# A cross-network recommendation kernel on one core: the first group's seven shifted-row loads in buffers of their own, and a changed order of waits around the scratch writes

## What is computed

```python
x = x0                                   # e: [512, 40, 16]
for k in (k0, k1, k2):                   # k0: [128,40,40], k1, k2: [128,128,40]
    x = jnp.einsum('bhd,bmd,ohm->bod', x, x0, k)
    outputs.append(jnp.sum(x, axis=-1))
z = jnp.concatenate(outputs, axis=1)
h = jnp.concatenate([z, dense_ctx], axis=1)
h = relu(h @ W_top1 + b_top1); h = relu(h @ W_top2 + b_top2)
y = h @ W_top3
```

## Time and profile before

| | |
|---|---|
| time before, median of 3 runs (lowest to highest) | 703.82 us (703.36 to 705.27) |
| the profiled execution: time, span | 706.33 us, 704.4 us |
| TensorE busy | 651.3 us, 92% of the span |
| VectorE busy | 619.2 us, 88% |
| ScalarE busy | 554.1 us, 79% |
| GpSimd busy | 321.0 us, 46% |
| start of the first layer 1 matmul | 41.48 us |
| mean granted TensorE clock | 0.995 of full speed |

### The profile page before, as it was taken

How to read it: one execution, slowest core, us unless ns; L and a number is a source line. 1 busy time by engine, 2 the same in 40 slices (tenths; PEclk the granted TensorE clock), 3 DMA queues, 4 the chain that set the end, 5 groups by cost and what they waited for, 6 DMA issues and landing times.

```text
span 704.4 us, 11705 instructions
## 1 busy us (share of the span) xinstructions
PE 651.3 (92%) x2502; PEld 463.7 (66%) x2502; DVE 619.2 (88%) x1355; ACT 554.1 (79%) x1950; POOL 321.0 (46%) x250
## 2 busy tenths in 40 slices
PE   0389999999989999999999999999999999999998
PEld 0157776776767777777667777777777767765573
DVE  2559999999999999999899999999999999988390
ACT  2158888888888988888788888898888898889383
POOL 6645564636364655556463647465545611110000
PEclk9989999999999999999999999999999999999999
DMA  6431212121312122221213130212222122400000
GB/s 212 115 88 49 76 46 80 45 80 33 92 21 56 53 52 72 50 74 46 80 34 91 31 89 22 62 48 51 74 49 75 45 79 65 174 3 0 30 2 0
DMA packets 56671, 43.00 MB, mean 61 GB/s; under 512 B 37007, under 2 KB 40335, under 8 KB 56352
## 3 DMA queue, kind: packets, MB, share of 16 engines
q1 hardware_dynamic: 51488, 41.08, 19.7%
q0 software_dynamic: 5120, 1.32, 2.3%
HBM read 40.41 MB, written 1.97 MB: 60 GB/s over the span
## 4 chain that ended last, share of the span: by engine, by line
PE 76%; DVE 14%; issue 5%; DMA 2%; POOL 1%; DVEq 1%; SPq 0%; ACT 0%
PE Y L572 17%; PE Y L574 16%; PE Y L573 16%; PE X L539 14%; DVE sums L487 4%; PE GB L546 4%; DVE sums L436 2%; DVE sums L431 2%; DVE sums L449 2%; PE X L610 1%; POOL x0g L288 1%; DMA pairs<-scratch 1%; DVE x1lo L420 1%; PE X L612 1%; PE X L611 1%
## 5 line engine op out<-in xcount | busy, mean ns | idle before, releaser
L372 ACT ACTIVATE sums<-Y,xtok 128x128 f32<-128x128 f32 x1792 | 493.4, 395 | 91.1 <-PE Y L574 91.0
L572 PE MATMUL Y<-k1lo,x1hi 128*128 128x512 f32 x640 | 315.5, 493 | 20.3 <-DVE sums L487 17.1
L574 PE MATMUL Y<-k1hi,x1lo 128*128 128x512 f32 x640 | 253.5, 396 | 0.0
L573 PE MATMUL Y<-k1hi,x1hi 128*128 128x512 f32 x640 | 252.8, 395 | 0.0
L487 DVE SCALAR_TENSOR_TENSOR sums<-Y,xtok,sums 128x128 f32<-128x128 f32 x768 | 229.4, 341 | 24.2 <-PE Y L574 21.9
L317 POOL TENSOR_TENSOR diag<-xtok,mask 128x320 f32<-128x320 f32 x64 | 103.9, 1624 | 267.2 <-PE GB L546 267.0
L288 POOL DMA_INDIRECT x0g<-in_table,rows_now x160 | 199.2, 1245 | 42.2 <-issue 38.6
L572 PEld LDWEIGHTS Y<-k1lo,x1hi 128*128 128x128 f32 x640 | 120.6, 188 | 82.2 <-DVE sums L487 27.8
L573 PEld LDWEIGHTS Y<-k1hi,x1hi 128*128 128x128 f32 x640 | 121.1, 189 | 50.6 <-issue 25.3
L539 PE MATMUL X<-pairs,w 120*128 120x512 f32 x224 | 116.9, 604 | 29.8 <-DVE pairs L416 29.8
L574 PEld LDWEIGHTS Y<-k1hi,x1lo 128*128 128x128 f32 x640 | 120.7, 189 | 29.2
(11 more groups left out here) (64 smaller groups left out, 249.3 us busy)
## 6 DMA issues: line engine op xcount, KB each, us to landing
pairs<-scratch SPq DMA_DIRECT2D x112, 240.0 KB
A<-scratch SPq DMA_DIRECT2D x16, 240.0 KB
k1raw<-in_k SPq DMA_DIRECT2D x1, 2560.0 KB, 10.6
x0g<-in_table,rows_now POOLq DMA_INDIRECT x160, 3.2
k2s<-in_k SPq DMA_DIRECT2D x1, 2560.0 KB, 9.1
scratch<-x0g SPq DMA_DIRECT2D x96, 20.0 KB, 1.7
pairs<-in_w SPq DMA_DIRECT2D x3, 256.0 KB, 3.0
w2s<-in_w SPq DMA_DIRECT2D x1, 512.0 KB, 4.0
```

Of the source, the lines that this page charges most:

```text
L372: ins = nc.scalar.activation(sums[tile % 2][:, k * O:(k + 1) * O], Y[(NCH * tile + c) % YB][:, i * O:(i + 1) * O], ACT.Copy, scale=xtok[sl ...
L572: nc.tensor.matmul(y, hi[:, tok], k1lo[:, cols], start=True, stop=False)
L573: nc.tensor.matmul(y, hi[:, tok], k1hi[:, cols], start=False, stop=False)
L574: nc.tensor.matmul(y, lo[:, tok], k1hi[:, cols], start=False, stop=True).then_inc(s_y, 1)
```

## The change

Four edits. (1) In `spread(0, -1)` the seven chunks of the first group are loaded into seven buffers `first0` to `first6`, which lie in bytes of `G` that are not yet in use, so SyncE waits for no matmul between them. (2) For the first group `A3` waits only for the four writes of rows 0 to 39; the two repeated pieces have a semaphore of their own (`s_again`), for which SyncE waits after it has issued `A3`. (3) For all later groups SyncE waits, ahead of the two writes of repeated rows (40 to 59), until all of layer 0 of the group before is done (`s_l0 >= NC0 * g`); `A3` and the chunks stand behind that wait. (4) `chunk` counts buffers from group 1 on, since the first group no longer uses `pairs`.

```diff
@@ def chunk
-    k = NC0 * (slot + 1) + c
-    return GPB * NC0 * u + k, k % NR, GPB * NC0 // NR * u + k // NR
+    number, k = NC0 * (GPB * u + slot + 1) + c, NC0 * slot + c
+    return number, k % NR, GPB * NC0 // NR * u + k // NR
@@ buffers
+        first = [over("G", f"first{c}", [P, GROUP], skip=4 * (NCH * BANK + 2 * NC0 * O + c * GROUP))
+                 for c in range(NC0)]
@@ SyncE, spread
-                for q in range(FQ):
-                    for first in range(q * GF, ROLLS, M):
-                        sp.dma_start(scratch[par, first:first + GF, :].rearrange("f (b d) -> b f d", d=D),
-                                     x0g[par][q * GS:(q + 1) * GS, :, :]).then_inc(s_scratch, 16)
-                sp.wait_ge(s_scratch, 16 * (ROLLS // GF) * (g + 1))
+                for row in range(0, ROLLS, GF):
+                    q = row % M // GF
+                    if row == M and slot >= 0:
+                        sp.wait_ge(s_l0, NC0 * g)
+                    sp.dma_start(scratch[par, row:row + GF, :].rearrange("f (b d) -> b f d", d=D),
+                                 x0g[par][q * GS:(q + 1) * GS, :, :]).then_inc(
+                                     s_again if slot < 0 and row >= M else s_scratch, 16)
+                sp.wait_ge(s_scratch, 16 * (ROLLS // GF * g + FQ))
                 sp.dma_start(A3[par][0:PR, :], rows(0, 0)).then_inc(s_a3, 16)
+                if slot < 0:
+                    sp.wait_ge(s_again, 16 * (ROLLS // GF - FQ))
                 for c in range(NC0):
+                    if slot < 0:
+                        sp.dma_start(first[c][0:PR, :], rows(KC * c, 1)).then_inc(s_first[c], 16)
+                        continue
                     n, buf, _ = chunk(u, slot, c)
-                    if slot >= 0 or c >= NR:
-                        sp.wait_ge(s_l0, n - NR + 1)
+                    sp.wait_ge(s_l0, n - NR + 1)
                     sp.dma_start(pairs[buf][0:PR, :], rows(KC * c, 1)).then_inc(s_roll[buf], 16)
@@ VectorE, prod steps (TensorE's l0 steps read the same buffer)
+                    if slot < 0:
+                        rolled = first[int(step[4:])]
+                        dve.wait_ge(s_first[int(step[4:])], 16)
+                    else:
+                        _, buf, fills = chunk(u, slot, int(step[4:]))
+                        rolled = pairs[buf]
+                        dve.wait_ge(s_roll[buf], 16 * (fills + 1))
+                    nc.vector.tensor_tensor(rolled[0:PR, :], rolled[0:PR, :], A3[par][0:PR, :],
                                             ALU.mult).then_inc(s_prod, 1)
```

More of the change, by code:

```diff
@@ L191, in build @@
         s_xtok = sem("xtok_ready")
-        s_scratch, s_a3 = sem("scratch_written"), sem("a3_in")
+        s_scratch, s_again, s_a3 = sem("scratch_written"), sem("scratch_written_again"), sem("a3_in")
+        s_first = [sem(f"first_in{c}") for c in range(NC0)]
         s_roll = [sem(f"rolled_in{i}") for i in range(NR)]
@@ L412, in prep @@
                 if step[:4] == "prod":
-                    _, buf, fills = chunk(u, slot, int(step[4:]))
                     dve.wait_ge(s_a3, 16 * (g + 1))
-                    dve.wait_ge(s_roll[buf], 16 * (fills + 1))
-                    nc.vector.tensor_tensor(pairs[buf][0:PR, :], pairs[buf][0:PR, :], A3[par][0:PR, :],
+                    if slot < 0:
[6 more added lines that the diff above has]
+                    nc.vector.tensor_tensor(rolled[0:PR, :], rolled[0:PR, :], A3[par][0:PR, :],
                                             ALU.mult).then_inc(s_prod, 1)
@@ L538, in prep @@
                     pe.wait_ge(s_prod, n + 1)
-                    nc.tensor.matmul(X1[:, :], w0[:, c * O:(c + 1) * O], pairs[buf][0:PR, :],
+                    rolled = pairs[buf] if slot >= 0 else first[c]
+                    nc.tensor.matmul(X1[:, :], w0[:, c * O:(c + 1) * O], rolled[0:PR, :],
                                      start=(c == 0), stop=(c == NC0 - 1)).then_inc(s_l0, 1)
```

## The result

The changed kernel took 708.97 us (median of 14 runs, 704.0 to 712.97) against 704.13 us for the kernel before (14 runs, 702.83 to 707.25). The ratio is 1.0056, with a 95% interval from 1.0035 to 1.0077. I had forecast 698.0 us. The start did become earlier, much as worked out; the time was lost in the middle, at a place that the prediction never looked at.

What follows compares the result with a forecast made beforehand. TensorE's list, with a little of VectorE's, was taken to bound the tiles. Seven buffers with early `A3` 4.6, clock 1.4, less 0.2 for the new wait, gave 5.8 us: from 703.8 to 698.0 us, range 697.0 to 701.3.

Steps and rivals of the forecast that it cites:

- What bounds the kernel: In the tiles TensorE's list sets the cost; time saved in the first 41 us moves everything forward one for one.
- Part 1: At the start, `A3` goes out at 20.8 and the first chunk at 21.8, 0.95 us earlier; the added wait is hidden.
- Part 2: In the first group, seven buffers make TensorE the limit; `l0_6` ends at 35.4 against 40.00, a gain of 4.6 us.
- Part 3: At the start of layer 1, TensorE no longer runs at half clock, a gain of 1.4 us; called the least certain step.
- the dip: TensorE's granted clock at 0.50 from 38 to 44.5 us in the profile before; its staying was a rival, chance 0.16.
- Part 4: In later groups, SyncE's new wait leaves 3.6 us to spare; only group 1 is charged, 0.1 to 0.2 us.
- The rival on the slower side: In 14 groups VectorE stands at `prod0` because `A3` and chunk 0 come late; 703 to 708 us, chance 0.05.

Runs made afterwards that it cites:

- e5: Changed kernel with the wait for layer 0 only in the first slot (slot 0) of a loop body; 708.62 us, ratio 1.004 to the kernel before.
- e10: Changed kernel without the wait for layer 0, plus five 240 KB copies that no product waits for, issued at the jump back; 708.07 us, ratio 1.0028.
- e12: The kernel before with the loop over bodies written out; 700.77 us, ratio 0.9937 to the kernel before.
- e2: The kernel before with only the wait for layer 0 ahead of the repeated rows added (scratch writes reordered to allow it); 712.09 us, ratio 1.0097.
- e1: Changed kernel without the wait for layer 0 ahead of the repeated rows, first group's `A3` with its own semaphore; 701.78 us, ratio 0.9954 to the kernel before.
- e4: Changed kernel with the wait for layer 0 in all slots of a loop body but the last; 709.45 us, ratio 1.0058 to the kernel before.
- e3: Changed kernel with the wait for layer 0 only in the last slot of a loop body, first group's `A3` with its own semaphore; 702.24 us, ratio 0.9955.
- e6: Changed kernel with the wait for layer 0 in slots 1 to 3 only, first group's `A3` with its own semaphore; 702.49 us, ratio 0.9949.
- e7: Changed kernel, all waits kept, with the loop over bodies written out four times; 697.61 us, ratio 0.9881 to the kernel before.
- e8: Changed kernel without the wait for layer 0 and with the loop over bodies written out; 698.87 us, ratio 0.9894 to the kernel before.
- e11: Changed kernel without the wait for layer 0, first group's `A3` waiting for all six scratch writes again; 703.22 us, ratio 0.9968 to the kernel before.

## Why the prediction was wrong

- **What bounds the kernel.** Right for the groups inside a body. Wrong in "unless the tiles themselves are disturbed" being left without a search: I looked at one later group (the one at 303 us) and took it for all 15. The two periods across a jump already stood out before, by 1.4 us each, and the very view of the earlier trace rows had an entry for them (waiter, releaser, total us, times, longest):

```profile
DVE sums L444 <- issue: 2.9, 2, 1.5
```

- **Part 1, early `A3`.** I had 20.8 and 21.8; the profile has 21.30 and 22.26, and `A3` in the other runs with this start lies between 20.43 and 21.31. Right in mechanism, and hidden as said. Its worth of 0.95 us was not told apart from noise.
- **Part 2, seven buffers.** TensorE was the limit of the start, without a gap, as said. (The 4.50 us that I called waiting for a load were the load's own; TensorE stood still for 2.26 us between its pairs. It doesn't enter the sum, which follows the ends of the pairs.) `l0_6` ended at 36.93 and not 35.4: half a microsecond from the landing of the scratch writes, and six pairs in 6.94 us where I had 5.9, since the clock rose later. In e5 they took 5.58 us and layer 1 began at 36.74; in e10 6.87 and 38.08. The moment of the rise differs from run to run, so this term has a spread of over 1 us.
- **Part 3, the dip.** It was gone in the changed kernel, so the term of 1.4 us held for these two profiles. But e12 and e2 keep the old start, with two waits for loads of about a microsecond, and begin layer 1 at 39.51 and 39.78 with the clock up. And of the 78 runs of the kernel before beside the experiments, 29 had a mean granted clock of 1.000, which leaves no room for a dip. So it belonged to the profiled execution; waits of this size alone don't bring it, and what did is open. The agreement that I read from the trace was one execution's. I had subtracted 5.8 us "as a fixed piece from each" run; about 2 us of the start (41.48 against 39.51) and the 1.4 us within layer 1 were not fixed. Without the wait the change gains 0.46% (e1), 3.2 us.
- **Part 4, the new wait. This is the step that failed.** It had the wait at 0.1 to 0.2 us. I asked only whether the products would have to wait for their chunks, and that answer was right: group 1's `prod0` stood 0.47 us, for which I had 0.3, and no later product waited. The price came from what else the moved transfers meet, the jump back of the engines' lists: 6.1 us over the two periods of the profiled runs, and 7.2 us between the medians of the kernel after (708.97) and of e1 (701.78), which were not taken side by side. The rival on the slower side had the wrong mechanism (lateness) and so the wrong test; 703 to 708 was near the result by chance.
- **The clock behind it.** A busy jump costs twice: the stall, and a lowered clock that follows it in most cases. The profiles show the place. At the ten quiet jumps the granted clock stayed at 1.00. At the ten busy ones it fell at eight: from 193 to 205 us it was 0.72 in e2, 0.86 in e4 and 0.72 in e5, but 1.00 in the kernel after and in e10; from 349 to 363 us it was 0.76 to 0.88 in all five. The runs agree: a mean granted clock of 0.993 or lower in 9 of 14 runs of the changed kernel, 3 of 7 in e2, 9 of 12 in e4, 6 of 10 in e5 and 9 of 10 in e10, against 7 of 78 for the kernel before, 1 of 12 in e1, and none in e3, e6, e7, e8, e11 and e12. The two changed runs at 1.000 took 704.2 us, so the stall alone ate the gain of the start; the five at 0.990 had a median of 710.5. In e2, though, three of the seven runs had 0.998 and took 711.0 to 712.1 us, so there most of the loss stood without the clock.
- **The tail.** The 3.4 us that the profiled run lost in the tail don't belong to the wait. From 640 to 664 us the clock was lowered in e1, e3, e6, e8 and e11 as well (0.86 to 0.93), whose jumps are quiet or gone, and not in e4 and e5. So it is in part by chance that the two profiles differ by as much as the medians (5.0 and 4.8 us).

## What to carry to other kernels

When a wait or a load is moved, list everything that its transfers will meet at the new time, the engines' jumps back in a loop among them. Follow one step through all iterations: a period that stands out is where the view of a typical iteration fails. Keep transfers away from the back jump, or write the loop out: the changed kernel written out, at 697.61 us (0.9881), is the fastest of all. A gain from the clock in one profiled execution is to be counted as a chance, not as a term.

## What the runs showed of the hardware

A jump back leaves VectorE idle for 1.3 to 1.5 us where the transfers are silent (9 GB/s) and for 3.0 to 4.4 us with 174 to 226 GB/s moving, whoever the data is for (e10's copies as well as the kernel's own loads). The instruction packets of the profile come in later there. TensorE's clock fell at eight of ten such busy jumps and at none of ten quiet ones. The same start ran with the granted clock down for nearly 7 us (from 38 us in the profile before) or not at all (e12, e2). And the loop written out, with a longer list for each engine, was faster by 0.6% (e12) and not slower.
